# Attention steps on TensorE: the PV matmuls of an older chunk put ahead of the score matmuls of the new one, under one set of waits

## What is computed

```python
Q, K, V = x·Wq + bq, x·Wk + bk, x·Wv + bv      # 16 heads of 64
scores  = where(causal, Q·K^T / sqrt(64), -inf)
o       = softmax(scores)·V                     # heads side by side
x = layernorm(x + o·Wo + bo)
h = silu(x·wg^T) * (x·wu^T)                     # int weights / 127, 3072 wide
x = layernorm(x + h·wd^T)
```

## Time and profile before

| | |
|---|---|
| median of 3 runs | 2095.82 us (2095.59 to 2096.98) |
| profiled execution, its own time | 2097.09 us |
| its span on the slowest core (core 3) | 2095.5 us |
| spans of the eight cores | 2084.1 to 2095.5 us |
| TensorE matmuls busy | 1728.3 us (82%), 8992 instructions |
| ScalarE busy | 927.8 us (44%) |
| VectorE busy | 680.2 us (32%) |
| exp L388 | 640 instructions, 1023 ns each |
| mask L399 | 256 instructions, 1224 ns each |

### The profile page before, as it was taken

One profiled execution on the slowest core, in us unless ns is written; L12 is line 12 of the kernel. 1 busy time (PEld: TensorE's weight loads), 2 busy tenths in 40 slices (PEclk: granted clock), 3 DMA queues, 4 the chain that ended last, 5 costly groups with the idle time before them and its releaser, 6 DMA issues. The chain is left out here.

```text
span 2095.5 us, 24644 instructions; the slowest of 8 cores (2084.1 to 2095.5 us)
## 1 busy us (share of the span) xinstructions
PE 1728.3 (82%) x8992; PEld 673.5 (32%) x8992; DVE 680.2 (32%) x792; ACT 927.8 (44%) x1174; POOL 94.0 (4%) x181
## 2 busy tenths in 40 slices
PE   1269897998988998989989886675599996899993
PEld 1144232252232442322522321221244441344440
DVE  1213254315252333542152524255221114212115
ACT  0013866936858738769468587223111103111103
POOL 2200000000000000000000000000111100111000
PEclk9689898999898998989998988877799998899995
DMA  8921000001000010000000001700344300344002
GB/s 143 141 31 21 1 1 11 1 1 21 1 11 1 1 20 2 1 11 1 1 0 1 1 1 15 130 17 1 61 81 80 62 1 36 85 81 81 1 1 80
DMA packets 30803, 64.64 MB, mean 31 GB/s; under 512 B 3808, under 2 KB 3936, under 8 KB 30048
## 3 DMA queue, kind: packets, MB, share of 16 engines
q0 software_dynamic: 25376, 52.44, 15.5%
q1 hardware_dynamic: 5312, 10.63, 1.5%
HBM read 107.10 MB, written 8.39 MB: 55 GB/s over the span
## 5 line engine op out<-in xcount | busy, mean ns | idle before, releaser
L388 ACT ACTIVATE PT<-pp 128x1024 bf16<-128x1024 f32 x640 | 627.9, 1023 | 189.5 <-PE pp L377 183.2
L399 DVE TENSOR_TENSOR PT<-PT,masks_sb 128x1024 bf16<-128x1024 bf16 x256 | 308.1, 1224 | 380.7 <-ACT PT L388 380.5
L419 PE MATMUL pso<-PT,V 128*64 128x512 bf16 x640 | 268.4, 419 | 50.9 <-DVE PT L399 33.4
L373 PE MATMUL pp<-Q2T,K2T 64*128 64x512 bf16 x640 | 262.7, 414 | 54.0 <-ACT PT L388 46.0
L422 PE MATMUL pso<-PT,V 128*64 128x512 bf16 x640 | 272.5, 426 | 0.0
L377 PE MATMUL pp<-Q2T,K2T 64*128 64x512 bf16 x640 | 263.8, 416 | 0.0
L428 PE MATMUL psd<-PT,onescol 128*1 128x512 bf16 x640 | 253.2, 396 | 0.0
L426 PE MATMUL psd<-PT,onescol 128*1 128x512 bf16 x640 | 253.1, 395 | 0.0
L296 PE MATMUL pp<-wv_sb,xT 128*128 128x256 bf16 x1024 | 136.5, 277 | 17.9 <-DMA wv_sb<-wv 14.8
L419 PEld LDWEIGHTS pso<-PT,V 128*64 128x64 bf16 x640 | 69.2, 108 | 215.5 <-issue 215.5
L373 PEld LDWEIGHTS pp<-Q2T,K2T 64*128 64x128 bf16 x640 | 58.9, 94 | 228.7 <-issue 228.7
(11 more groups left out here) (103 smaller groups left out, 1820.9 us busy)
## 6 DMA issues: line engine op xcount, KB each, us to landing
wgb<-wg POOLq DMA_DIRECT2D x48, 256.0 KB, 5.6
wub<-wu POOLq DMA_DIRECT2D x48, 256.0 KB, 6.5
stg<-x POOLq DMA_DIRECT2D x32, 256.0 KB, 15.2
y<-y SPq DMA_DIRECT2D x4, 2048.0 KB, 6.9
wd_sb<-wd POOLq DMA_DIRECT2D x4, 1536.0 KB, 11.4
stg<-xq POOLq DMA_DIRECT2D x16, 256.0 KB, 11.5
masks_sb<-mk SPq DMA_DIRECT2D x1, 2048.0 KB, 12.2
wq_sb<-wq POOLq DMA_DIRECT2D x8, 256.0 KB, 4.5
```

Source lines behind the costliest of these rows:

```text
L373: e.matmul(pp[par][:, 0:512], K2T[0:64, kc * 128:(kc + 1) * 128], Q2T[0:64, t * 512:(t + 1) * 512], start=True, stop=True)
L388: pool_cons.append(st('act', lambda e, par=par, gpt=gpt: e.activation(PT[:, gpt, :], pp[par][:], AF.Exp, scale=SCALE), waits=exp_waits, in ...
L399: msnap = st('dve', lambda e, gpt=gpt, t=t, rel=rel: e.tensor_mul(PT[:, gpt, :].rearrange("p (h q) -> p h q", h=2), PT[:, gpt, :].rearrang ...
L419: e.matmul(ps_o[opar][0:64, :], V2[:, kc, ppar * 128:ppar * 128 + 64], PT[:, gpt, 0:512], start=first, stop=last)
```

## The change

The two steps of a stream become one step, `fused`. Its waits are those of both, put in front of all its matmuls, and within it PV and den of chunk `j - 2` come ahead of S of chunk `j`. Increments stay where the work ends: the one for PV on the last den matmul, the one for S on the last S matmul. Where only one half exists (no PV at `j` of 0 and 1, no S after a tile's last chunk), the step has that half alone, with its waits alone. The lines between, for exp and mask, stay. All matmuls, exps, masks and buffers are the same.

```diff
+                    pk = j - 2
+                    do_s = j < nkc
+                    do_pv = 0 <= pk < nkc
+                    if not (do_s or do_pv):
+                        continue
+                    waits = []
+                    if do_pv:
+                        waits.append(pv_ready[(t, pk)])
+                        if pk == 0:
+                            waits += [('s_dve_on', last_on[opar]),
+                                      ('s_dve_rs', last_rs[opar])]
+                    if do_s:
...
+                        waits += [(f's_plc{u % 2}', u // 2)] + kq_ready
...
+                    def fused(e, t=t, nkc=nkc, pk=pk, do_s=do_s, do_pv=do_pv,
...
+                        inst = None
+                        if do_pv:
+                            e.matmul(ps_o[opar][0:64, :],
...
+                            inst = e.matmul(ps_den[opar][64:65, :], onescol[:],
...
+                            inst.then_inc(pvsem, 1)
+                        if do_s:
                             e.matmul(pp[par][:, 0:512],
...
+                            inst = e.matmul(pp[par][:, 512:1024],
...
+                        return inst
+
+                    if do_s:
+                        user_done.append(st('pe', fused, waits=waits,
                                             inc=('s_pe_user', 1)))
-                        user_done.append(st('pe', smm,
-                                            waits=[(f's_plc{u % 2}', u // 2)] + kq_ready,
-                                            inc=('s_pe_user', 1)))
...
-                    def pvmm(e, kc=pk, opar=opar, gpt=slot_of[(t, pk)], ppar=ppar,
-                             nkc=nkc):
...
-                    pv_done[(t, pk)] = st('pe', pvmm, waits=pv_waits, inc=('s_pe_pv', 1))
+                    else:
+                        st('pe', fused, waits=waits)
```

More of the change, by code:

```diff
@@ L366, in build_full @@
                     opar = t % 2
-                    if j < nkc:
+                    pk = j - 2
[10 more added lines that the diff above has]
+                    if do_s:
                         kc = j
@@ L370, in build_full @@
                         gpt = g % NSLOT
-                        def smm(e, kc=kc, t=t, par=par):
+                        waits += [(f's_plc{u % 2}', u // 2)] + kq_ready
+                    if do_pv:
+                        mk.c['s_pe_pv'] += 1
+                        pv_done[(t, pk)] = mk.c['s_pe_pv']
+                    pvsem = mk.sem('s_pe_pv')
+                    def fused(e, t=t, nkc=nkc, pk=pk, do_s=do_s, do_pv=do_pv,
+                              kc=j, par=u % 2, gpt=g % NSLOT, opar=opar, ppar=ppar,
+                              gpv=(slot_of[(t, pk)] if do_pv else 0), pvsem=pvsem):
+                        inst = None
+                        if do_pv:
+                            first, last = pk == 0, pk == nkc - 1
+                            e.matmul(ps_o[opar][0:64, :],
+                                     V2[:, pk, ppar * 128:ppar * 128 + 64],
+                                     PT[:, gpv, 0:512], start=first, stop=last)
+                            e.matmul(ps_o[opar][64:128, :],
+                                     V2[:, pk, ppar * 128 + 64:ppar * 128 + 128],
+                                     PT[:, gpv, 512:1024], start=first, stop=last,
+                                     tile_position=(0, 64), skip_group_check=True)
+                            e.matmul(ps_den[opar][0:1, :], onescol[:],
+                                     PT[:, gpv, 0:512], start=first, stop=last)
+                            inst = e.matmul(ps_den[opar][64:65, :], onescol[:],
+                                            PT[:, gpv, 512:1024], start=first,
+                                            stop=last, tile_position=(0, 64),
+                                            skip_group_check=True)
+                            inst.then_inc(pvsem, 1)
+                        if do_s:
                             e.matmul(pp[par][:, 0:512],
@@ L376, in smm @@
                                      start=True, stop=True)
-                            return e.matmul(pp[par][:, 512:1024],
+                            inst = e.matmul(pp[par][:, 512:1024],
                                             K2T[64:128, kc * 128:(kc + 1) * 128],
                                             Q2T[64:128, t * 512:(t + 1) * 512],
-                                            start=True, stop=True, tile_position=(64, 0))
-                        user_done.append(st('pe', smm,
-                                            waits=[(f's_plc{u % 2}', u // 2)] + kq_ready,
+                                            start=True, stop=True,
+                                            tile_position=(64, 0))
+                        return inst
+                    if do_s:
+                        user_done.append(st('pe', fused, waits=waits,
                                             inc=('s_pe_user', 1)))
```

## The result

The changed kernel takes 2284.88 us (median of 8 runs), the kernel before 2095.59 (median of 7); the ratio is 1.090, 95% interval 1.089 to 1.092. It is slower by 189 us, where 158 were forecast. In some executions of every kernel one die had a lower granted clock and took some per cent longer; times and ratios from here on are of the other executions.

What follows compares the result with a forecast made beforehand. TensorE was taken to bound the two-stream part, VectorE's masks the tails. Per pair 1.0 + 1.5 + 1.6 + 7.8 + 2 x 3.9 = 19.7 us, over eight pairs 157.6, giving 2253 us; range 2235 to 2290.

Steps and rivals of the forecast that it cites:

- Two-stream part: Attention with both streams: PV and den enter a buffer's round, 1.18 us per unit; loses 1.5 and 7.8 us per pair.
- No gain from the boundary that goes away: Between a stream's two steps: removing the boundary saves nothing, as den to S takes 0.31 us, S to PV 0.32.
- Starts: Start of each group: PV ahead delays S, by 1.0 us in the first group and 1.6 in the second.
- Tails: Stream B's last chunks: the mask enters a buffer's round, 3.70 us for two units; loss 3.9 us per tail.
- The clock: TensorE's clock in the new tails: taken to cost nothing, with 44 us left to the range.
- the table's row on what follows a group: From a group's last S to the next group's first: forecast 0 per pair, measured 1.7 us.
- The bound from above: If every tail runs at low clock: 31 us in tails, 13 in the stage behind each pair, together 44.
- the rival with the clock falling in the tails: Tails: the clock falls, up to 2297 us, 2275 with half of them falling; chance 0.22.
- that rival: Two-stream part: the clock goes up and down; 2332 us if half of the steps fell; chance 0.06.

## Why the prediction came out as it did

*Two-stream part.* Right in mechanism and size: 2.36 us for two units was forecast from four rows, and is what the profile shows. Only the form differs: not 0.2 us ahead of each of 350 PVs, but 0.35 ahead of every second, 198 in all. The two experiments that undo one half each show that it takes both halves, order and merged wait, as the buffer's round had it.

*No gain from the boundary that goes away.* Nothing in the runs speaks against it: with S first and one step for two, the two-stream part is at 0.97, as with two steps.

*Starts.* Forecast 1.0 and 1.6 us. With the two-stream parts they make 2.0 and 9.2 per pair for 2.5 and 9.4. In the second group the first PV waits for the norm (1.23 us, until 583.02) and S comes behind it, at 584.11, as described.

*Tails.* The mechanism is right: with the mask out of the round some 70 us come back, and with S ahead in the tail as before, some 108. The size of the round, 3.70, was short by the 0.11 that the second wait adds (3.80), 5 us in all; the experiment with swapped waits shows it, though there it comes back in the two-stream part. Where A's last step was one without a wait, the step behind it had one of 0.35 us that the layout didn't have, so by its steps a tail at full clock takes 15.8 to 16.0 us for the 15.5 forecast.

*The clock.* This is the term that was mis-sized. "I take nothing, as its steps of work are like those of the old tail" was the step that failed. The steps of work are like the old ones, but every second gap of the new tail, 1.14 us, is longer than any of the old one's, which went up to 0.7. The new tails fell: they took 16.9 us on the mean, and all but one of the 16 more than the 16.0 of the one that kept its clock. That is 15 to 18 us in the tails, and with the 14 of the table's row on what follows a group (8 x 1.7), where the work is the old one, 29 to 32 us for the clock. With the tails kept busy, some 25 of them came back. The bound from above was 44, and so the rival with the clock falling in the tails, at 2275 to 2297, is the case that came about. The forecast's own range of 2230 to 2276 doesn't hold 2284.9; the wider one, 2235 to 2290, does, since it took in most of those 44 us for a fall that the forecast itself didn't expect. In the two-stream part gaps of 0.35 us at every second step left the granted clock at 1.00, so that rival fell. Gaps of 0.58 and 1.14 us in turn, in the tails, brought it down in all but one of them, to a mean of 0.80 and 0.84. The Trainium skill's rule (TensorE: Matmul & The Clock Gate, section "A second HAM failure mode: psum-queue depth-cycling") has the clock oscillate where TensorE idles for moments between groups of matmuls; the tails agree with it, the two-stream part doesn't.

Added up: 158 forecast, less the 6 us (8 x 0.7) by which starts and two-stream parts came out lower, 5 for the second wait, 29 to 32 for the clock, and up to 3 for the first step of the tails: 189.

What stays open: which gap exactly makes the clock fall, and why one tail of the 16, with the same gaps, kept it.

## What to carry to other kernels

Put into an in-order queue, a piece of work that is ready belongs behind the piece that feeds the next engine, not ahead of it, and above all not under its wait: follow one buffer round through all engines, add up what now stands in it, and compare with the work of the busiest engine in that time. A wait that is merged is harmless where the work behind it isn't in the round, and ruinous where it is. When a change opens gaps on TensorE, price the low clock in the gaps and in what follows them, and take the price from rows on both sides.

## What the hardware showed beyond that

- A pair of matmuls that follows a pair of the same shape starts 0.22 to 0.24 us behind it, behind one of another shape 0.31 to 0.34. Grouping by shape took 21 us off, 1%. The Trainium skill says in TensorEngine Tiling (Array Packing), section "Key Properties", that changing the tiling mode drains the engine; these rows agree, and put some 0.1 us on it. They don't tell, though, whether PV and den, both on 128 rows of the array, are in different modes: den starts 0.34 us behind PV all the same.
- A wait that is long met, taken behind the one that binds, costs TensorE 0.11 us: mask to PV 0.25 for 0.14 in the tail, and with the waits swapped 2.47 for 2.36 us in the masked rounds of the two-stream part.
- More matmuls made a kernel faster: repeated scores that fill TensorE's waits kept its clock up in the tails; of the 34 us less than the changed kernel some 25 are the clock's.
